# Four constant multiplications ahead of two of the four waits for probabilities, in both graph-attention stages

## The reference

```
e[i,j]  = leaky_relu(h[i]·a1 + h[j]·a2, slope 0.2)     512 x 512
e[i,j]  = -infinity where adj[i,j] says no edge
p[i,:]  = softmax over j of e[i,:]
x[i,:] += sum over j of p[i,j] h[j,:]
```

## Time and profile before

| | |
|---|---|
| median of three executions | 4651.02 us (4650.3 to 4657.94) |
| the profiled execution's own time | 4630.8 us |
| its span, first to last instruction | 4628.9 us |
| mean granted clock of PE over the span | 0.817 of full speed |
| gat2, main part | 2671.5 to 2961 us of the span, granted clock 0.79 |
| gat3, main part | 3425.9 to 3607 us of the span, granted clock 1.00 |

### The profile page before, as it was taken

One profiled execution on the slowest core, in us unless ns is written; L12 is line 12 of the kernel. 1 busy time (PEld: TensorE's weight loads), 2 busy tenths in 40 slices (PEclk: granted clock), 3 DMA queues, 4 the chain that ended last, 5 costly groups with the idle time before them and its releaser, 6 DMA issues. The chain is left out here.

```text
span 4628.9 us, 82058 instructions
## 1 busy us (share of the span) xinstructions
PE 3536.2 (76%) x24355; PEld 2162.1 (47%) x24355; DVE 2789.2 (60%) x10800; ACT 2067.1 (45%) x5218; POOL 1736.8 (38%) x2184
## 2 busy tenths in 40 slices
PE   3999995666666649999987876379847788874994
PEld 1333334444444423333365666357636555542663
DVE  5777756555555566677577767612277576752444
ACT  1777773322222217777632365334347444431221
POOL 3555520000000013433294337744446445434445
PEclk7999995555555559999998987689969999886997
DMA  4444429500000023343100122144342000002445
GB/s 129 125 129 134 127 66 378 245 0 0 0 0 0 0 80 112 116 125 115 54 2 2 35 64 82 37 133 143 119 145 83 1 11 20 15 15 76 131 130 165
DMA packets 235820, 386.93 MB, mean 84 GB/s; under 512 B 25344, under 2 KB 157568, under 8 KB 227136
## 3 DMA queue, kind: packets, MB, share of 16 engines
q1 hardware_dynamic: 217152, 345.83, 23.3%
q0 software_dynamic: 18432, 38.31, 2.4%
HBM read 210.70 MB, written 173.34 MB: 83 GB/s over the span
## 5 line engine op out<-in xcount | busy, mean ns | idle before, releaser
L1482 DVE CUSTOM_DVE_ANT_0 mha_seen<-mha_score,mha_mask 128x512 f32<-128x512 f32 x1024 | 683.3, 688 | 381.6 <-PE mha_score L1245 375.3
L1386 ACT ACTIVATE mha_prob<-mha_turned 128x512 f32<-128x512 f32 x1024 | 587.7, 602 | 308.6 <-PE mha_turned L1259 300.6
L1638 PE MATMUL lstm_gates<-lstm_h_part,lstm_w_part 128*128 128x16 f16 x4608 | 277.2, 179 | 327.9 <-DVE lstm_h_part L1853 324.4
L1245 PE MATMUL mha_score<-mha_k_rows,mha_q_rows 96*128 96x512 bf16 x1024 | 401.1, 394 | 58.9 <-DMA mha_k_rows<-split_rows 38.8
L3192 POOL DMA_INDIRECT expert_rows<-expert_y,expert_target x320 | 307.4, 960 | 367.2 <-DVE expert_y L3338 150.8
L1638 PEld LDWEIGHTS lstm_gates<-lstm_h_part,lstm_w_part 128*128 128x128 f16 x4608 | 215.8, 107 | 481.0 <-DVE lstm_h_part L1853 475.5
L1259 PE MATMUL mha_turned<-mha_q_rows,mha_k_rows 99*128 99x512 bf16 x1024 | 391.3, 383 | 7.6 <-ACT mha_turned L1370 6.5
L1585 POOL TENSOR_TENSOR core_mid<-lstm_hist,lstm_per_unit 128x128 f32 x64 | 29.5, 460 | 886.4 <-DVE lstm_hist L1854 886.4
L1725 ACT ACTIVATE lstm_act<-lstm_gates 128x48 f32<-128x48 f32 x512 | 108.0, 211 | 428.2 <-PE lstm_gates L1638 428.2
L1258 PE MATMUL mha_turned<-mha_maskT,core_ident_bf 128*128 128x512 bf16 x768 | 295.5, 385 | 0.5 <-ACT mha_prob L1386 0.3
L3230 PEld LDWEIGHTS expert_out_ps<-expert_w,expert_hid 128*128 128x128 f32 (+1 forms) x2240 | 262.4, 191 | 38.7 <-issue 35.6
(11 more groups left out here) (558 smaller groups left out, 8854.2 us busy)
## 6 DMA issues: line engine op xcount, KB each, us to landing
routed_rows<-lstm_blank SPq DMA_DIRECT2D x66, 1056.0 KB, 26.9
gat_adj_raw<-adj SPq DMA_DIRECT2D x32, 1024.0 KB, 5.4
mha_q_rows<-split_rows SPq DMA_DIRECT2D x64, 384.0 KB, 4.0
mha_k_rows<-split_rows SPq DMA_DIRECT2D x64, 384.0 KB, 4.9
expert_x<-routed_rows SPq DMA_DIRECT2D x80, 264.0 KB
expert_w<-weights SPq DMA_DIRECT2D x80, 256.0 KB
core_params<-adj SPq DMA_DIRECT2D x16, 1024.0 KB, 5.8
combine_pair<-expert_rows SPq DMA_DIRECT2D x32, 512.0 KB, 4.8
```

The costliest lines, as they stand in the source:

```text
L1245: pe.matmul(score[n % 2][:, :], rows[0][s][0:ROWS, h, t * P:(t + 1) * P], rows[1][s][0:ROWS, h, :], start=True, stop=True).then_inc(S["sco ...
L1386: act.activation(prob[:, n % RING, :], turned[n % 3][:, :], ACT.Exp, scale=-1.0).then_inc(S["prob_ready"], 1)
L1482: dve.tensor_tensor_reduce(seen[n % 2][:, :], score[n % 2][:, :], mask[1 - s][:, t, :], 1.0, 3e38, ALU.add, ALU.min, low[g][:, t, j:j + 1] ...
L1638: return pe.matmul(out, w[:, g * P:(g + 1) * P], h_part[:, part, :], start=False, stop=stop, skip_group_check=True)
```

## The change

A tile `still` of 128 x 512 bfloat16 zeros is added to both stages. POOL fills it once at the start of the stage, and PE waits for that once. In `back(b, t)` the wait for `copied` now stands first; for t = 0 and t = 2, four matrix products of the bfloat16 identity with `still` follow, which write zeros to the bank `tpose[t % 2]`; then comes the wait for `prob_ready` and the four transposes, which write the same bank over. Nothing reads the zeros.

```
+        still = m.sb("still", [P, N], BF16)
...
+            pool.memset(still[:, :], 0.0).then_inc(S["still_set"], 1)
             need(pool, "stat_done", STATS[False])
...
             def back(b, t):
+                need(pe, "copied", T * b + t - 1)
+                if t in (0, 2):
+                    for n in range(4):
+                        pe.matmul(tpose[t % 2][:, :], core.ident_bf[:, :], still[:, :], start=True, stop=True)
                 need(pe, "prob_ready", T * b + t + 1)
-                need(pe, "copied", T * b + t - 1)
                 for u in range(T):
                     ins = pe.transpose(tpose[t % 2][:, u * P:(u + 1) * P], z[b % 2][:, t, u * P:(u + 1) * P], core.ident[:, :])
                 ins.then_inc(S["turned"], 1)
...
             need(pe, "wa_ready", 2)
+            need(pe, "still_set", 1)
```

More of the change, by code:

```diff
@@ L2758, in gat_stage @@
                  "xt_done", "xT_ready", "t_done", "s_done", "s_ready", "h_done", "h_ready", "masked", "max_chain", "max_ready", "leaky", "s_low", "low_ready",
-                 "prob_ready", "turned", "copied", "v_done", "rinv_ready", "upd_done", "stat_chain", "const_set", "stat_out", "power_set", "again_chain"]
+                 "prob_ready", "turned", "copied", "v_done", "rinv_ready", "upd_done", "stat_chain", "const_set", "stat_out", "power_set", "again_chain", "still_set"]
         S = {n: m.sem(n) for n in names + Router.NAMES}
```

## The result

The changed kernel takes 4670.17 us (median of 6 runs, 4668.52 to 4675.53) where the kernel before took 4650.07 us on the same chip (4644.75 to 4657.94): +20.1 us, ratio 1.0043 with a 95% interval of 1.0031 to 1.0054. That is slower, by more than the 0.2% that a measurement tells apart. It lies inside the range (4640 to 4672) and 12 us above the forecast of 4658.

What follows compares the result with a forecast made beforehand. PE, busiest at 76% and not always at full clock, sets the pace from back(b,1) to rows_in(b+2). Terms 12.3 + 2.7 - 7.0 = +8.0 us on 4651.0 gave 4659, rounded down to 4658; 8-in-10 range 4640 to 4672.

Steps and rivals of the forecast that it cites:

- Shorter wait ahead of back(b,1): PE's wait for the exponent before the transposes: the t = 0 group makes it 0.88 us shorter, in gat2 2.49 to 1.61.
- gat3: Second stage, clock full throughout: 0.15 us more per graph; with graphs 0 and 1 of gat2, 18 graphs, 2.7 us.
- The clock: gat2 graphs without a second wait: the shorter wait keeps the clock up more often, giving 7.0 us back (bounds 0 and 23.2).
- the work it pushes back then runs later, at full clock, and takes half; so the net is again 0.88: t = 2 group in gat2's graphs 2 to 15: 1.76 us at half clock still nets 0.88; 14 x 0.88 = 12.3 us.
- B: Rival: constant products do not keep the clock up, nothing comes back; +15 us, 4666, up to +27, 4678; chance 0.25.
- The rest costs nothing: Both stages: POOL's fill of still, PE's wait for it and the wait for copied add no time.
- The sum: Whole kernel: 12.3 + 2.7 - 7.0 = +8.0 us, carried to the median of 4651.0 and rounded down to 4658.
- its second half: B's further case in gat2: the clock also rises later, so the t = 2 group costs 1.76 us there; up to +27, 4678.
- The rule behind it: Trainium skill's rule used for B: transposes do not count as PE being busy, so graph 3's stretch stays at 2.49 us.
- C: Rival: clock stays up in gat2's eight graphs without a second wait, -8 us, 4643; with seven odd ones 4621; chance 0.15.
- the first half of its mechanism: C's first part: the clock stays up in all eight gat2 graphs without a second wait, 15 - 23.2 = -8 us.
- D: Rival: unseen slack behind gat2's router turn brings the 12.3 nearer to gat3's 2; 4650 or a little less; chance 0.1.

## Why the prediction came out as it did

**Shorter wait ahead of back(b,1): right.** Forecast 0.88 us less; 2.49 became 1.72 in gat2 and 0.95 became 0.18 in gat3, 0.77 less. Of the difference of 0.11 us, 0.09 is the swapped order of the waits (2.58 and 2.49 with nothing else changed).

**gat3: right in size, wrong in which group.** Forecast 0.15 us per graph, 0.08 of t = 0 and 0.11 of t = 2 less an overlap. Measured 0.114, all of it t = 0; with t = 2 alone the period stays 12.028. The first and the last graph of a stage were missing from the sum. No wait stands ahead of the first and PE runs at half clock, so the first group shows nearly whole, 1.4 to 1.5 us in each stage; the group at t = 2 shows with 1.1 us in gat3's first period and 0.9 behind back(15,1).

**The clock: right, and larger than put.** Forecast: a wait of 1.6 us instead of 2.5 mostly keeps the clock. In the first measurement it was 1.00 through graphs 0 to 4, and a share of 0.82 against 0.83 forecast. With t = 0 alone the clock stays up in every period that ends at an odd graph. Its median is 9.4 us better than that of the kernel without products relative to before (-5.1 against +4.3), and it carries 4.2 us of costs (1.3 in gat3's main part, 1.4 and 1.5 at the two starts), so the clock gave about 13.6 us where I put 7.0. The scale that the 7.0 came from was wrong at one end. It had 2.49 us of wait as what always lets the clock fall; in the kernel before, run again, four periods behind such a wait ran at 1.00 throughout. That "always" was the pattern of one execution. With t = 2 beside it that gain is gone: 269.70 us with both groups, 269.45 with t = 2 alone.

**The step that failed: "the work it pushes back then runs later, at full clock, and takes half; so the net is again 0.88".** Of the 14 groups at 0.88 us the ones in graphs with the clock up cost 0.75, a little under the term. The ones behind the counts cost 3 us: the group itself is 1.70 us at half clock, as B had it for the case that the clock rises later, and the counts come 1.9 us later, because a graph longer by 0.75 us moves POOL's elementwise work onto DVE's small router steps. No rival named this second part. I had asked what stands behind the group on PE and not what the shift does between the two other engines.

**The rest costs nothing: not confirmed.** With the tile alone 5.7 us appear, with no products 4.3 us, and neither interval reaches 1. It is not the order of the waits. The memset was put where POOL stood idle, but it holds up DVE, which POOL was waiting for, by 0.33 us; that the rest is another pattern of falls is likely and not shown.

**The sum.** On the second set of chips the change is +10.2 us where +8 was forecast: more clock gained, more lost behind the counts, 4 us that came with the tile. So it is near by terms that missed in both directions, and that is in part luck. In the first measurement another 10 us come with results that reach ACT late while POOL scatters; that 4670.17 still lies inside the range is owed to the range's width and not to a term in it. In its trace the periods that end at an odd graph lose 36.7 us against the same kernel elsewhere (109.0 and 72.3), while before loses 11.7 there (83.0 and 71.3). That the lateness in gat2 grows with the change is what one trace of each kernel shows; it is there without the change too, 39 us in 13 waits in the attention behind gat3 (44 in 13 with the change). That the products make gat2 meet more of it was not tested, as no later run of the kernel before took 4650 us. It stays open.

**The rivals.** B had the sign, and its 4666 to 4678 hold the time of the first measurement, but its reason, that constant products do not keep the clock up, is refuted by both the t = 0 kernel and the one with products in the wait; only its second half, 1.76 us at half clock, is seen. The rule behind it (transposes do not count as busy) is not decided. I compared unlike stretches: by the rule graph 3 goes from 2.49 + 0.44 + 0.44 = 3.4 us to 1.72 + 0.44 + 0.44 = 2.6, and not to the 2.49 that was a wait alone. The clock stayed up at 2.6; but in the kernel before, run again, it also stayed up four times at 3.4, so the length of the stretch does not decide by itself, with the transposes or without. C did not come in the changed kernel, but the first half of its mechanism did with t = 0 alone and with the products in the wait: no fall in a period without counts. (Its 3.2 us for an odd graph should read 6.88 / 2 = 3.4; nothing hangs on it.) D is refuted for gat2: 0.75 us per group.

## What to carry to other kernels

Put filler into a wait that something else ends, or ahead of one that can swallow it: five products inside the long wait gained 10.7 us, a group ahead of ready work with that wait behind it gained 5.1, and the same with a second group in the stretch where PE sets the pace lost 10. Ask of each added microsecond not only who waits behind it but which instructions of two other engines it moves on top of each other. Compare with a kernel that has the edit's scaffolding without its work: 4 to 6 us here came with the scaffolding. And take no "always" for the clock from one profile: the same kernel had 15 falls in one and 10 in another.

## What the hardware showed that I had not expected

- Products of a tile of zeros keep the granted clock at 1.00 (five in the long wait: 11.38 us of PE work in a 14.0 us graph, no fall in a period without counts; half clock 39 us of the main part, 96 without products).
- DVE instructions of 0.2 to 0.7 us take 1.1 to 1.8 us when POOL's elementwise instruction of 1.05 us runs beside them, and one of 0.20 us takes 0.53 beside POOL's memset; DVE's masks of 0.69 us do not lengthen.
- In the first measurement ACT went on up to 4.4 us after the records of the PE work that it needed had ended in gat2's main part, within 1.6 us of the end of one of POOL's scatters (up to 2.0 us in the kernel before); on the three other chips never. The same kernel takes 4650 us there and 4551 here.
